# Value products of two units in one group: four buffers of transposed probabilities and one evacuation for each pair of units

## What is computed

```python
light = light_local_attn(h, ...)        # 8 heads of 64, windows of 128 rows: softmax(q k^T) v, then @ wo
scores_q, idx_q = route(h, q_tok, 128)  # 50 iterations of coordinate descent, then top-k
scores_kv, idx_kv = route(h, kv_tok, 256)
routed = heavy_attn(h[idx_q], h[idx_kv], scores_kv, ...)   # 8 heads of 64, 128 queries over 256 keys
return light + scatter(idx_q, routed * scores_q)
```

## Time and profile before

| | us |
|---|---|
| median of 3 runs (569.96 to 571.25) | 570.33 |
| span of the profiled execution | 567.3 |
| TensorE matmul busy | 516.8 (91%) |
| ScalarE busy | 407.2 (72%) |
| VectorE busy | 399.1 (70%) |
| GpSimd busy | 229.4 (40%) |

### The profile page before, as it was taken

The page is one execution under the profiler, slowest core; times in us unless marked ns, Lnnn a source line. Parts: engine busy times, 40 slices in busy tenths (PEclk is TensorE's granted clock), DMA queues, the critical chain, the costliest instruction groups (busy, mean ns, idle before and its releaser), DMA issues.

```text
span 567.3 us, 14031 instructions
## 1 busy us (share of the span) xinstructions
PE 516.8 (91%) x3955; PEld 428.7 (76%) x3955; DVE 399.1 (70%) x1360; ACT 407.2 (72%) x1544; POOL 229.4 (40%) x281
## 2 busy tenths in 40 slices
PE   3588778659999999999999799999999999999996
PEld 1476656547888888888888587888888888888885
DVE  6459999957888888888886974555655665565652
ACT  2378999667888898989888686666566566566562
POOL 6236677733333333333332332433333344333342
PEclk9999999878999999999999999999999999999999
DMA  9820000101000000000000000111111111111000
GB/s 242 333 87 10 30 28 19 65 21 38 21 20 19 20 21 19 18 18 18 20 20 20 20 30 29 47 39 39 39 38 39 38 37 37 39 44 50 24 10 28
DMA packets 25037, 24.58 MB, mean 43 GB/s; under 512 B 2752, under 2 KB 24016, under 8 KB 24736
## 3 DMA queue, kind: packets, MB, share of 16 engines
q1 hardware_dynamic: 23808, 22.32, 12.0%
q0 software_dynamic: 432, 1.31, 0.7%
q10 hardware_dynamic: 752, 0.40, 0.3%
HBM read 11.41 MB, written 4.23 MB: 28 GB/s over the span
## 4 chain that ended last, share of the span: by engine, by line
PE 73%; DVE 3%; issue 2%; ACT 1%; POOL 1%; POOLq 0%; ACTq 0%; DVEq 0%
PE bank L711 13%; PE bank L713 10%; PE bank L712 10%; PE bank L894 6%; PE bank L1010 6%; PE bank L965 6%; PE bank L997 5%; PE bank L912 5%; PE bank L880 5%; PE bank L1026 2%; PE bank L944 2%; PE bank L1035 1%; PE bank L955 1%; ACT pr L629 1%; DVE left L1336 0%
## 5 line engine op out<-in xcount | busy, mean ns | idle before, releaser
L466 POOL TENSOR_TENSOR pr<-pr,rinv 128x512 f32<-128x512 f32 x64 | 66.6, 1040 | 142.5 <-DVE rinv L1311 142.5
L481 POOL TENSOR_TENSOR pr<-pr,rinv 128x512 f32<-128x512 f32 x64 | 66.6, 1040 | 130.4 <-DVE rinv L1427 130.3
L629 ACT ACTIVATE pr<-bank,nmx 128x128 f32<-128x128 f32 x256 | 90.0, 370 | 5.0 <-DVE nmx L1305 5.0
L681 ACT ACTIVATE pr<-bank,nmx 128x256 f32<-128x256 f32 x128 | 59.4, 472 | 26.6 <-DVE nmx L1421 26.6
L1305 DVE TENSOR_REDUCE nmx<-bank 128x4 f32<-128x512 f32 x64 | 43.9, 686 | 31.2 <-PE bank L713 31.1
L629 ACT ACTIVATION_READ_ACCUMULATOR pr<-bank,nmx 128x1 f32 x256 | 54.0, 211 | 0.0
L1421 DVE TENSOR_REDUCE nmx<-bank 128x2 f32<-128x512 f32 x64 | 43.8, 685 | 10.0 <-PE bank L713 10.0
L894 PE MATMUL bank<-pt,V 128*64 128x128 f32 x512 | 42.1, 285 | 1.0 <-ACT pt L650 0.7
L880 PE MATMUL bank<-ident,pr 128*128 128x128 f32 x256 | 39.0, 275 | 4.3 <-POOL pr L466 4.3
L1010 PE MATMUL bank<-pt,V 128*64 128x128 f32 x512 | 42.1, 285 | 0.0
L965 PE MATMUL bank<-xq,T_w 128*128 128x128 f32 x256 | 40.7, 282 | 0.4 <-ACT xq L658 0.4
(11 more groups left out here) (253 smaller groups left out, 1573.6 us busy)
## 6 DMA issues: line engine op xcount, KB each, us to landing
mod_bc<-mod_rows_scratch SPq DMA_DIRECT2D x1, 3072.0 KB, 11.3
X<-in_L_attn_x SPq DMA_DIRECT2D x4, 512.0 KB, 8.7
xh_scratch<-xhs SPq DMA_DIRECT2D x16, 128.0 KB, 1.7
xt0hi<-XT_hi SPq DMA_DIRECT2D x16, 128.0 KB, 2.0
xt0lo<-XT_lo SPq DMA_DIRECT2D x16, 128.0 KB, 2.0
xt1hi<-XT_hi SPq DMA_DIRECT2D x16, 128.0 KB, 2.0
xt1lo<-XT_lo SPq DMA_DIRECT2D x16, 128.0 KB, 2.0
xh<-xh_scratch SPq DMA_DIRECT2D x16, 128.0 KB, 2.2
```

The lines of the kernel that those rows point to most:

```text
L466: pool.tensor_tensor(q, q, rinv[k % 4][:, :, None].broadcast_to([P, 4, P]), ALU.mult)\
L481: pool.tensor_tensor(q, q, rinv[k % 4][:, 0:2, None].broadcast_to([P, 2, N]), ALU.mult)\
L629: act.activation(pr[k % 4][:, i * P:(i + 1) * P], ps[2 + k % 2][:, i * P:(i + 1) * P], ACT.Exp, bias=nmx[k % 4][:, i:i + 1], accum_out=sum ...
L681: act.activation(pr[k % 4][:, i * N:(i + 1) * N], ps[2 + k % 2][:, i * N:(i + 1) * N], ACT.Exp, bias=nmx[k % 4][:, i:i + 1], accum_out=sum ...
```

## The change

The value products of an even and the following odd unit are issued together in the odd unit's step, sixteen rows instead of two times eight. In the light phase the pair is one window (eight heads), which fills all 512 columns of bank 6; in the heavy phase the pair is four heads and fills 256 columns. Even steps issue no value products. The transposed probabilities of both units must be kept until then, so `pt` has four buffers. Bank 6 is evacuated once a pair, by one instruction of 512 (light, ScalarE) or 256 columns (heavy, VectorE). The semaphores `Op` and `oT` count pairs, and all waits on them are rewritten. The number of products and their operands stay the same, and so do the lags and the order of stages.

```diff
-        pt = [sb(f"pt{i}", [P, 512]) for i in two]
+        pt = [sb(f"pt{i}", [P, 512]) for i in range(4)]
...
             def o_evac(p, k):
-                g, b, j = 8 * p + k, 2 * p + k // 4, k % 4
-                w, half = j // 2, j % 2
-                act.wait_ge(lt["Op"], g + 1)
-                at_least(act, lt["outp"], 2 * b + w - 1)
-                act.activation(oT[w][:, 2 * half:2 * half + 2, :],
-                               ps[6][:, 0:2 * P].rearrange("p (q t) -> p q t", q=2), ACT.Copy).then_inc(lt["oT"], 1)
+                if k % 2 == 0:
+                    return
+                window, w = 4 * p + k // 2, k % 4 // 2
+                act.wait_ge(lt["Op"], window + 1)
+                at_least(act, lt["outp"], window - 1)
+                act.activation(oT[w][:, :, :], ps[6][:, :].rearrange("p (q t) -> p q t", q=4), ACT.Copy)\
+                    .then_inc(lt["oT"], 1)
...
-                at_least(dve, lt["Op"], g - 1)
-                dve.tensor_copy(pt[k % 2][:, :], ps[4 + k % 2][:, :]).then_inc(lt["PT"], 1)
+                at_least(dve, lt["Op"], 4 * p + k // 2 - 1)
+                dve.tensor_copy(pt[k % 4][:, :], ps[4 + k % 2][:, :]).then_inc(lt["PT"], 1)
...
             def values(p, k):
-                g, b, j, par = 8 * p + k, 2 * p + k // 4, k % 4, b_par(k)
-                w, half = j // 2, j % 2
+                if k % 2 == 0:
+                    return
+                g, window, w, par = 8 * p + k, 4 * p + k // 2, k % 4 // 2, b_par(k)
                 pe.wait_ge(lt["PT"], g + 1)
-                pe.wait_ge(lt["v"], 2 * b + w + 1)
-                if is_unit(g, 0):
+                pe.wait_ge(lt["v"], window + 1)
+                if is_unit(g, 1):
                     pe.wait_ge(r["rows"], 1)
-                at_least(pe, lt["oT"], g)
-                for q in range(2):
+                at_least(pe, lt["oT"], window)
+                for q in range(4):
                     for i in range(2):
-                        h = 4 * half + 2 * q + i
+                        h = 2 * q + i
                         mm = pe.matmul(ps[6][i * DH:(i + 1) * DH, q * P:(q + 1) * P],
                                        V[par][:, w, h * DH:(h + 1) * DH],
-                                       pt[k % 2][:, (2 * q + i) * P:(2 * q + i + 1) * P], start=True, stop=True)
+                                       pt[k % 4 - 1 + q // 2][:, (h % 4) * P:(h % 4 + 1) * P], start=True, stop=True)
                 mm.then_inc(lt["Op"], 1)
...
             def values_h(p, k):
+                if k % 2 == 0:
+                    return
                 g, b, j, par = 8 * p + k, 2 * p + k // 4, k % 4, b_par(k)
                 pe.wait_ge(hv["PT"], g + 1)
                 pe.wait_ge(hv["v"], 2 * b + 2)
...
-                for w in range(C):
-                    for i in range(2):
-                        h = 2 * j + i
-                        mm = pe.matmul(ps[6][i * DH:(i + 1) * DH, 0:NQ], V[par][:, w, h * DH:(h + 1) * DH],
-                                       pt[k % 2][:, (2 * i + w) * P:(2 * i + w + 1) * P],
-                                       start=(w == 0), stop=(w == C - 1))
+                for n in range(2):
+                    for w in range(C):
+                        for i in range(2):
+                            h = 2 * (j - 1 + n) + i
+                            mm = pe.matmul(ps[6][i * DH:(i + 1) * DH, n * NQ:(n + 1) * NQ],
+                                           V[par][:, w, h * DH:(h + 1) * DH],
+                                           pt[k % 4 - 1 + n][:, (2 * i + w) * P:(2 * i + w + 1) * P],
+                                           start=(w == 0), stop=(w == C - 1))
                 mm.then_inc(hv["Op"], 1)
...
             def o_evac_h(p, k):
+                if k % 2 == 0:
+                    return
                 g, b, j, par = 8 * p + k, 2 * p + k // 4, k % 4, b_par(k)
-                dve.wait_ge(hv["Op"], g + 1)
-                if is_unit(g, 0):
+                dve.wait_ge(hv["Op"], 4 * p + k // 2 + 1)
+                if is_unit(g, 1):
                     dve.wait_ge(lt["outp"], 2 * B)
                 at_least(dve, hv["outp"], b - 1)
-                dve.tensor_copy(oT[par][:, j, :], ps[6][:, 0:NQ]).then_inc(hv["oT"], 1)
+                dve.tensor_copy(oT[par][:, j - 1:j + 1, :], ps[6][:, 0:2 * NQ].rearrange("p (q t) -> p q t", q=2))\
+                    .then_inc(hv["oT"], 1)
```

More of the change, by code:

```diff
@@ L647, in pt_evac_act @@
                 act.wait_ge(lt["PTp"], g + 1)
-                act.wait_ge(lt["Op"], g - 1)
+                act.wait_ge(lt["Op"], 4 * p + k // 2 - 1)
                 act.wait_ge(lt["PT"], g)
-                act.activation(pt[k % 2][:, :], ps[4 + k % 2][:, :], ACT.Copy).then_inc(lt["PT"], 1)
+                act.activation(pt[k % 4][:, :], ps[4 + k % 2][:, :], ACT.Copy).then_inc(lt["PT"], 1)
             def xq_evac(p, k):
@@ L695, in pt_evac_h @@
                 if is_unit(g, 0):
-                    act.wait_ge(lt["Op"], 8 * PAIRS)
-                at_least(act, hv["Op"], g - 1)
-                act.activation(pt[k % 2][:, :], ps[4 + k % 2][:, :], ACT.Copy).then_inc(hv["PT"], 1)
+                    act.wait_ge(lt["Op"], 4 * PAIRS)
+                at_least(act, hv["Op"], 4 * p + k // 2 - 1)
+                act.activation(pt[k % 4][:, :], ps[4 + k % 2][:, :], ACT.Copy).then_inc(hv["PT"], 1)
             run_phases(act, ([(2, qk_evac), (1, h_evac), (6, squares), (3, exps_a), (5, ln2), (0, ln1), (3, pt_evac_a),
@@ L902, in out_light @@
                 g, b, w = 8 * p + k, 2 * p + k // 4, k % 4 // 2
-                pe.wait_ge(lt["oT"], g + 1)
+                pe.wait_ge(lt["oT"], 2 * b + w + 1)
                 if is_unit(g, 1):
@@ L1003, in values_h @@
                 pe.wait_ge(hv["v"], 2 * b + 2)
-                if is_unit(g, 0):
-                    pe.wait_ge(lt["oT"], 8 * PAIRS)
-                at_least(pe, hv["oT"], g)
-                for w in range(C):
-                    for i in range(2):
-                        h = 2 * j + i
-                        mm = pe.matmul(ps[6][i * DH:(i + 1) * DH, 0:NQ], V[par][:, w, h * DH:(h + 1) * DH],
-                                       pt[k % 2][:, (2 * i + w) * P:(2 * i + w + 1) * P],
-                                       start=(w == 0), stop=(w == C - 1))
+                if is_unit(g, 1):
+                    pe.wait_ge(lt["oT"], 4 * PAIRS)
+                at_least(pe, hv["oT"], 4 * p + k // 2)
+                for n in range(2):
[6 more added lines that the diff above has]
+                                           start=(w == 0), stop=(w == C - 1))
                 mm.then_inc(hv["Op"], 1)
@@ L1017, in out_heavy @@
                     return
-                g, b, par = 8 * p + k, 2 * p + k // 4, b_par(k)
-                pe.wait_ge(hv["oT"], g + 1)
+                b, par = 2 * p + k // 4, b_par(k)
+                pe.wait_ge(hv["oT"], 2 * b + 2)
                 pe.wait_ge(hv["xq"], min(b + 4, B) if isinstance(b, int) else b + 4)
@@ L1411, in v_evac_h @@
                 if is_unit(b, 0, 1):
-                    dve.wait_ge(lt["Op"], 4 * (B - 1 + b))
-                at_least(dve, hv["Op"], 4 * (b - 1))
+                    dve.wait_ge(lt["Op"], 2 * (B - 1 + b))
+                at_least(dve, hv["Op"], 2 * (b - 1))
                 dve.tensor_scalar(V[par][:, w, :], ps[7][:, :], selT[:, 0, w, bass.ds(B + b, 1)], None, ALU.mult)\
```

2 lines of the change are left out of this document (1 added, 1 removed).

## The result

The changed kernel takes 549.89 us (median of 4 runs, 549.35 to 552.05) against 570.14 for the kernel before in the same session (569.52 to 571.25): a ratio of 0.9643, 95% interval 0.9617 to 0.9669. The profiled execution spans 547.6 us instead of 567.3, 19.7 less; the forecast was 19.6 less and 550.7 us.

The account below looks back on a forecast made before the run. TensorE's queue was taken to bound both loops, with gaps around each value group. Gains of 8.4 + 0.7 + 2.1 + 8.4 = 19.6 us gave 567.3 - 19.6 + 3.0 = 550.7 us, range 546 to 560.

Parts of the forecast that it names:

- Part 1: TensorE's value groups: each pair loses one entry, exit and slow first product, 0.35 us a light pair, 0.29 a heavy one.
- The pace of the second eight: Second half of a sixteen-row group: between 0 and 0.25 us extra, taken at 0.
- a rule against its sum: Group ends: if the increment alone makes the gap, 0.06 us for each of 64 groups, 4 us, 566 in all.
- Where it lands: Gain by stretch: before 144 us 0.7, light loop 8.4, between the loops 2.1, heavy loop 8.4; sum 19.6 us.
- The last pairs: Last three pairs, in the drain: between 3 x -0.44 and 3 x 0.29 us, taken at 0.
- The passage between the loops: From 309 to 360 us, six pairs: 2.1 us gained, between ends of -2.6 and all 5.6 idle us recovered.
- Part 2: Short even steps: 0.2 us left before the light j = 3 projection, 0.27 before the heavy gather; unevenness priced at nothing.
- Parts 3 and 4: Four buffers with later waits, and one evacuation a pair on ScalarE (0.60 us) or VectorE (0.40): both priced at 0.
- A: Light loop: another engine takes over, half the light gain goes, 556 us; 15%.
- B: Value groups: gaps belong to the increment or every eight rows, not the change of shape; 564 us or no change; 7%.
- D: Even steps don't close up while odd ones grow by 0.44 us: slower, in full 27 us more, 597; 4%.

Follow-up runs that it names:

- e3: Changed kernel with the sixteen value rows cut into two eights, 128*128 products between, still one increment and one evacuation a pair: 568.66 us, ratio 0.9958.
- e4: Changed kernel, sixteen rows left whole, but two semaphore increments and two evacuations a pair: 550.42 us, ratio 0.9641.
- e7: Changed kernel with VectorE's copy of the transposed probabilities put ahead of U's low part in light steps: 560.96 us, ratio 0.9837.
- quads: Changed kernel with heavy value products of four units in one group of 32 rows, G placed three ways (e5, e6, e10): 558.50, 555.43 and 549.55 us.
- e5: Changed kernel with heavy value products of four units in one group of 32 rows, one evacuation of 512 columns: 558.50 us, ratio 0.9794.
- e6: e5 with VectorE's G moved ahead of its copy of V: 555.43 us, ratio 0.9738.
- e10: e5 with the next sequence's G made in the step before, ahead of the reciprocal: 549.55 us, ratio 0.9613.

## Why the prediction was right

**Part 1, the gap per group.** Right in its mechanism and size. A light pair was put at 0.35; 24 pairs gave 8.3. A heavy pair was put at 0.29 and gave 0.31, so that term was 0.6 short. The other even step, with gather behind the group, had been given the same price without a sum of its own; it shrinks by 0.78 and 0.70 in turns (from 1.34 to 0.56 and 0.64 us, last product of the scores to the transposes), which makes 0.30 on average and leaves most of the 0.6 untraced. The pace of the second eight, which no row showed, was taken at no extra and has none. That the gap belongs to the group as one of another kind than its neighbours, and neither to the increment nor to every eight rows, was argued from rows; e3 and e4 show it. That the kind is the weights' shape still rests on rows. "TensorEngine Tiling (Array Packing)" in the Trainium skill, section "Key Properties", says that a change of tiling mode drains the engine and a change of tile doesn't; this trace agrees, with 0.33 instead of 0.23 at entry, 0.15 at exit, and no gap inside a group, whose products alternate between the two halves of the columns. The prediction weighed, as a rule against its sum, the tail that the Trainium skill, "TensorE: Matmul & The Clock Gate", section "The cost: per-tile semaphore tail", puts on each increment; in a full queue e4 shows none of it, with 0.9641 against 0.9643.

**Where it lands.** The light loop's 24 pairs: right. The heavy loop's 29: 9.0 instead of 8.4. The last pairs were taken at 0 and gave some 0.3, inside their bounds. The passage between the loops is the term that was wrong: 2.1 forecast and 1.0 measured (for one pair more), of which the half clock in that one execution took 0.3. 2.1 lay inside both ends, but the idle 5.6 us of the earlier trace rows said already that TensorE's queue isn't what ends there, and I priced its gaps in full all the same. The trace of before even had the projection waiting 0.30 for U's low part in this passage, so one even step's 0.78 could not be gained. The misses, 1.1 too much there and about 1.2 too little at the start (which is within its scatter), in the heavy loop and in the drain, cancel; that the sum came out within 0.1 is luck.

**Part 2, uneven steps.** Right for pairs in the loops: 0.21 left where 0.2 was put, and for gather 0.25 where 0.27 was put:

```profile
505.41 0.48 DVE L1402 TENSOR_SCALAR G<-iota,pos 128x128 f32<-128x128 f32 x2
506.14 0.68 PE L946 MATMUL bank<-G,xh 128*128 128x128 f32 x4
```

G ends at 505.89. e7 shows that the light margin is real, 0.16 of it usable, and that a lack costs more than its own length, by the 0.11 of the slow product behind a wait. The price named in the prediction (1.6 us for each 0.1) left both out: in the light loop alone e7 lost 6.8 in 12 periods, where 0.4 each would be 4.8. The margin was worked out for a step of the loop; in the passage there was none. The quads show the same for the heavy side: a step that was to close up by 1.1 us met three bounds one after another (G behind V, G beside GpSimd, the transposes behind GpSimd).

**Parts 3 and 4.** No matmul of the changed kernel waits from 144 to 298 and from 361 to 530 us, so the later waits cost nothing in the loops, and the fewer evacuations gave nothing that shows (e4). The merged evacuations take what was put: ScalarE 597 ns for 128x512 (0.60 put), VectorE 414 ns for 128x256 (0.40 put).

**The rivals.** A (another engine takes over) didn't happen in the loops, but with 0.21 and 0.25 us to spare; it did happen once in the passage, where VectorE's low part ended the even step, and e5 to e7 are what it looks like in the loops. B (the increment, or every eight rows) fell by e3 and e4. D, even steps that don't close up, is the mechanism that e5 shows: one gap a sequence less, 0.31, and yet a sequence that is 0.52 longer; with pairs it is that one step of the passage.

## What to carry to other kernels

When TensorE is full, read its timeline by distances between starts and look for a gap at each change of weight shape (128 to 64 columns and back); grouping the products of one shape saved one entry and exit a group, here 0.3 to 0.35 us, and twice as many increments and evacuations made no difference that shows. Price such a gap only in stretches where TensorE shows no idle time; elsewhere look first for what ends each step that is to close up, in the trace of before. Before making groups longer, write down for the step that gets shorter what must still fit into it, with the margin in us: 0.2 was enough for pairs in the loops, and the quads that overran it lost more than they won.

## What the runs showed of the hardware beyond that

VectorE's comparison that makes G (both operands and result in SBUF) is slowed by GpSimd. Shortest/median/longest ns of one half, in the changed kernel, in e6 and in e10, over 400 to 500 us:

```profile
L1402 DVE TENSOR_SCALAR G<-iota,pos x16: 275/280/283, 405.3 to 493.0; 128x128 f32<-128x128 f32 x16
```

```profile
L1411 DVE TENSOR_SCALAR G<-iota,pos x16: 265/685/1104, 405.9 to 496.2; 128x128 f32<-128x128 f32 x16
```

```profile
L1418 DVE TENSOR_SCALAR G<-iota,pos x16: 276/279/282, 403.4 to 490.3; 128x128 f32<-128x128 f32 x16
```

The second half of each pair in e6 starts within 0.02 us of GpSimd's 1.04 and ends 0.08 after them. VectorE's copy of V out of a PSUM bank isn't slowed beside the same GpSimd instruction (e10: 0.73 to 0.75 us beside it, 0.75 without):

```profile
441.07 0.73 DVE L1437 TENSOR_SCALAR V<-bank,selT 128x512 f32<-128x512 f32 x1
441.24 1.04 POOL L488 TENSOR_TENSOR pr<-pr,rinv 128x512 f32<-128x512 f32 x1 [1.11 <-DVE rinv L1449]
```

The Trainium skill, "VectorE: DVE Perf Modes", section "Two Vector instructions with no wait between them", names a second SBUF read interface that some VectorE instructions use and that is shared with GpSimd. These rows agree with that; that it is this interface which holds G was not tested apart.
